# The sums of a graph attention kept row by row on VectorE, with the division given to GpSimd

## The reference

```
xl = (x @ Wl.T + bl).reshape(n, H, C)             # H = 4 heads of C = 32
...
p = jnp.exp(e - m[dst])
z = jax.ops.segment_sum(p, dst, num_segments=n)
alpha = p / (z[dst] + 1e-16)
out = jax.ops.segment_sum(xl[src] * alpha[:, :, None], dst, num_segments=n)
...
h = jax.nn.elu(h)                                  # then the second attention
```

## Time and profile before

| | |
|---|---|
| time, median of 3 runs | 6555.59 us (6553.88 to 6563.34) |
| span of the profiled execution, first to last instruction (no other time of its own is known) | 8635.1 us |
| DVE busy in the span | 4326.1 us (50%) |
| POOL busy | 4305.3 us (50%) |
| PE busy | 4016.2 us (47%) |
| ACT busy | 2282.2 us (26%) |
| mean granted TensorE clock | 0.650 |

### The profile page before, as it was taken

One profiled execution on the slowest core, in us unless ns is written; L12 is line 12 of the kernel. 1 busy time (PEld: TensorE's weight loads), 2 busy tenths in 40 slices (PEclk: granted clock), 3 DMA queues, 4 the chain that ended last, 5 costly groups with the idle time before them and its releaser, 6 DMA issues. The chain is left out here.

```text
span 8635.1 us, 76490 instructions
## 1 busy us (share of the span) xinstructions
PE 4016.2 (47%) x19708; PEld 2671.9 (31%) x19708; DVE 4326.1 (50%) x14882; ACT 2282.2 (26%) x5999; POOL 4305.3 (50%) x4026
## 2 busy tenths in 40 slices
PE   1111158312888825654563664342465476567000
PEld 0000034101555514443442443332344355233000
DVE  3010069301999944434432553565244698677553
ACT  0000000001777621110110333354111133799000
POOL 5777720575000046546555674774555100888577
PEclk8555589655999955555555555555666666798555
DMA  1111100000222222222222343343122144555222
GB/s 42 47 46 47 47 19 0 21 1 5 103 113 107 99 70 79 69 73 64 69 68 63 112 128 112 94 139 112 44 68 68 77 161 163 125 146 138 76 82 77
DMA packets 413612, 684.96 MB, mean 79 GB/s; under 512 B 283685, under 2 KB 290444, under 8 KB 407978
## 3 DMA queue, kind: packets, MB, share of 16 engines
q1 hardware_dynamic: 282410, 542.14, 17.7%
q0 software_dynamic: 130944, 140.05, 7.5%
HBM read 310.94 MB, written 373.78 MB: 79 GB/s over the span
## 5 line engine op out<-in xcount | busy, mean ns | idle before, releaser
L711 POOL DMA_INDIRECT G<-states,srcq x1568 | 1678.9, 1071 | 851.1 <-issue 479.5
L1133 DVE TENSOR_TENSOR_SCAN R<-same,R,G 128x28 f32<-128x28 f32 x4480 | 883.8, 265 | 622.1 <-issue 499.9
L1793 PE MATMUL PS<-ident,HH 128*128 128x128 f32 x2357 | 529.8, 376 | 1257.4 <-ACT AT L2063 373.2
L2063 ACT COPY AT<-PS 128x512 f32<-128x512 f32 (+1 forms) x494 | 283.7, 581 | 2467.3 <-remote 1375.1
L1793 PEld LDWEIGHTS PS<-ident,HH 128*128 128x128 f32 x2357 | 402.8, 205 | 1332.9 <-issue 409.9
L711 POOL DMA_INDIRECT EE<-node_info,srcq x392 | 394.4, 1006 | 545.0 <-DMA node_info<-XC 415.7
L1701 PE MATMUL PS<-R 128*128 128x392 f16 x784 | 283.0, 361 | 673.2 <-remote 375.7
L711 POOL DMA_INDIRECT G<-states,srci x392 | 406.7, 1038 | 321.0 <-ACT HH L2161 199.1
L1808 PEld LDWEIGHTS PS<-WD,AT 128*128 128x128 f32 x2358 | 505.8, 316 | 183.0 <-issue 182.7
L1808 PE MATMUL PS<-WD,AT 128*128 128x64 f32 x2358 | 560.6, 416 | 0.0
L824 POOL DMA_INDIRECT out_nodes<-O,dstq x392 | 430.9, 1099 | 188.2 <-issue 123.3
(11 more groups left out here) (412 smaller groups left out, 10157.6 us busy)
## 6 DMA issues: line engine op xcount, KB each, us to landing
states<-O SPq DMA_DIRECT2D x70, 896.0 KB, 3.6
HH<-states SPq DMA_DIRECT2D x56, 896.0 KB
total<-R SPq DMA_DIRECT2D x56, 896.0 KB
XB<-resid SPq DMA_DIRECT2D x42, 896.0 KB
states<-HH SPq DMA_DIRECT2D x28, 896.0 KB, 3.9
G<-states,srcq POOLq DMA_INDIRECT x1568
resid<-XB SPq DMA_DIRECT2D x28, 896.0 KB
xl_of_src<-O SPq DMA_DIRECT2D x14, 1792.0 KB
```

Of the source, the lines that this page charges most:

```text
L711: return pool.indirect_dma_start(to, None, table_, bass.IndirectOffsetOnAxis(ap=idx, axis=0), bounds_check=bound, oob_is_err=False).then_i ...
L1133: last = dve.tensor_tensor_scan(out=out_[:, order, f], data0=flags[:, order], data1=in_[:, order, f], initial=initial[:, f:f + 1], op0=ALU ...
L1793: last = pe.transpose(PS[:, 4 + k, q * P:(q + 1) * P], HH[:, b, (g * G4 + q) * D2:(g * G4 + q + 1) * D2], ident[:])
L2063: act.copy(AT[:, k, 0:n * P], PS[:, 4 + k, 0:n * P]).then_inc(s_copied, 1)
```

## The change

The turned layout goes. DVE weighs a chunk in place in G or XB, seven instructions of 128 x 512, and it does so one chunk ahead: `weigh(i + 1)`, then `sum_rows(i)`, then the seven elus of chunk i-1 in a row. `sum_rows` adds column by column, 28 instructions of 128 x 128, each waiting for the one before. R is now a pair of buffers, and the first column of a chunk takes its carry from the last column of the other. GpSimd divides in seven instructions of 128 x 512 (L869 of the changed program). The flags, their copies by ACT and two fills are gone. SP's program is untouched.

```diff
+            after("sum1")
+            for i in range(CHUNKS):
+                b = i % 2
+                if i >= 2:
+                    pool.wait_ge(s_st[b], before["sum1", "st"] + 16 * (i // 2))
+                    pool.wait_ge(s_turned, before["sum1", "group"] + GROUPS * (i - 1))
+                pool.wait_ge(s_scan, before["sum1", "scan"] + 1 + i)
+                for g in range(GROUPS):
+                    at = slice(g * G4 * D2, (g + 1) * G4 * D2)
+                    last = pool.tensor_tensor(head_rows(HH[:, b, at]), head_rows(R[:, b, at]), per_head(Ec, i * C + g * G4, G4), ALU.mult)
+                last.then_inc(s_ready, 1)
...
-            def weighted(i, b, between=None):
...
+            def weigh(i, b):
+
                 dve.wait_ge(s_ld[b], before["sum1", "ld"] + 16 * (i // 2 + 1))
...
+                for g in range(GROUPS):
+                    some = head_rows(XL[b][:, g * G4 * D2:(g + 1) * G4 * D2])
+                    last = tt(some, some, per_head(Ea, i * C + g * G4, G4), ALU.mult)
+                last.then_inc(s_weighed, 1)
+
+            def sum_rows(i, b):
+
                 if i >= 2:
...
+                    dve.wait_ge(s_ready, before["sum1", "ready"] + i - 1)
+                dve.wait_ge(s_weighed, i + 1)
+                for j in range(C):
+                    row_before = R[:, b, (j - 1) * D2:j * D2] if j else R[:, 1 - b, (C - 1) * D2:]
+                    row = dve.scalar_tensor_tensor(out=R[:, b, j * D2:(j + 1) * D2], in0=row_before, scalar=same[:, i * C + j:i * C + j + 1],
+                                                   in1=XL[b][:, j * D2:(j + 1) * D2], op0=ALU.mult, op1=ALU.add)
+                    if j < C - 1:
+                        step(row)
+                row.then_inc(s_scan, 1)
...
-            weighted(0, 0)
-            for i in range(1, CHUNKS):
-                weighted(i, i % 2, elus(i - 1, (i - 1) % 2))
+            weigh(0, 0)
+            for i in range(CHUNKS):
+                step.reset()
+                if i + 1 < CHUNKS:
+                    weigh(i + 1, (i + 1) % 2)
+                sum_rows(i, i % 2)
+                if i:
+                    for g in range(GROUPS):
+                        elu(i - 1, (i - 1) % 2, g)
```

More of the change, by code:

```diff
@@ L234, in build_program @@
         s_sm = sem("softmax_step")
[L235 to L239, removed]
+        s_weighed = sem("rows_weighed")
         s_last = sem("last_tails_known")
@@ L361, in build_program, with head_rows, per_head @@
         AHEAD = 2
+        def head_rows(t):
+            return t.rearrange("p (j h c) -> p j h c", h=HEADS, c=D2 // HEADS)
+        def per_head(e, first, n):
+            return e[:, :, first:first + n].rearrange("p h j -> p j h").unsqueeze(3).broadcast_to([P, n, HEADS, D2 // HEADS])
         XL = [t.rearrange("p b n -> p (b n)") for t in (G[:], XB[:])]
@@ L1497, in _ @@
             barrier()
-            def weighted(i, b, between=None):
-                step.reset()
+            def weigh(i, b):
                 dve.wait_ge(s_ld[b], before["sum1", "ld"] + 16 * (i // 2 + 1))
[L1504 to L1522, removed]
-                if i >= 2:
-                    dve.wait_ge(s_st[b], before["sum1", "st"] + 16 * (i // 2))
-                dve.wait_ge(s_scan, before["sum1", "scan"] + 1 + i)
[L1526 to L1530, removed]
@@ L1539, in elu @@
                                          op0=ALU.add, op1=ALU.max).then_inc(s_elu, 1)
[L1541 to L1545, removed]
-            dve.sem_inc(s_elu, AHEAD)
-            for k in range(2):
-                step(dve.memset(FLAGS[k], 0.0))
-            dve.nop().then_inc(s_flags, 1)
-            weighted(0, 0)
-            for i in range(1, CHUNKS):
-                weighted(i, i % 2, elus(i - 1, (i - 1) % 2))
+            dve.sem_inc(s_elu, AHEAD)
+            weigh(0, 0)
[7 more added lines that the diff above has]
+                        elu(i - 1, (i - 1) % 2, g)
             for g in range(GROUPS):
@@ L1926, in _ @@
             barrier()
-            pe.matmul(PS[:, 3, 0:D2], CARRY[:], FEATS[:, :, C - 1], start=True, stop=True).then_inc(s_carry, 1)
+            pe.matmul(PS[:, 3, 0:D2], CARRY[:], R[:, 1, (C - 1) * D2:], start=True, stop=True).then_inc(s_carry, 1)
             turn("sum1", CHUNKS, 0, 0, 1)
@@ L2190, in _ @@
                 act.sem_inc(s_rows[b], 32)
[L2192 to L2196, removed]
             def both_steps(i, it, b):
-                if i + 2 < CHUNKS:
-                    flags(i + 2)
                 for g in range(GROUPS + 2):
@@ L2205, in both_steps @@
                         second_operands("sum1", i, b, g - 2, it=it)
-            for i in range(2):
-                flags(i)
             for i in range(CHUNKS):
```

## The result

The changed kernel takes 6767.4 us (median of 4 runs, 6761.62 to 6774.58) against 6554.7 before (4 runs). The ratio is 1.033, with a 95% interval of 1.0313 to 1.0346: 213 us slower, where 180 were forecast.

The account below looks back on a forecast made before the run. DVE was taken to bound the stage. Turns of stall 15.1 + weighing 4.3 + rows 10.6 + elus 17 = 47.0 us against 30.9 made the stage 622 instead of 441.5: 6556 + 180 = 6736 us, range 6650 to 6830.

Parts of the forecast that it names:

- What bounds the stage: DVE bounds the stage before the change, busy 434 of 490 us, at 30.9 us a chunk.
- the saving of DVE's work: On DVE, 21.4 us a chunk removed and 14.9 added: 6.5 less by busy time, 90 us in all.
- The load is late: At a turn's first weighing, DVE waits for chunk i+2's load behind earlier products: 15.1 us, ends 11.1 and 20.2.
- The elus in a row: DVE's seven elus, with no other work between, go at PE's pace: 17 us a chunk, ends 14.3 and 21.5.
- the rival of the low clock: PE's clock stays low in every burst: elus 21.5 us instead of 17, twelve times, +54, 6790 us; chance 14%.
- the forecast stage: The whole stage, summed from the first load's landing: 622 us where it took 441.5, so +180.
- the forecast's own range: Range of kernel time for the main case, given 60%: 6700 to 6775 us.
- Weighing 4.3 and rows 10.6: DVE's added work a chunk: weighing in place 4.3 us, and 28 row sums 10.6 us, ends 9.0 and 10.9.
- GpSimd's division costs nothing on the path: GpSimd's seven division instructions, 0.6 to 1.59 us each, are hidden by a cover of 6.4 us each.
- The rival that GpSimd holds DVE up: GpSimd's division delays each of a turn's first two elus by up to 1.59 us: +38, 6774 us; chance 9%.
- The faster rival: At DVE's weighing the load isn't waited for: -27, 6528 us with elus at 14.3, +8 at 17; chance 6%.
- Carrying the stage's microseconds over in full: The stage's 180 us were added whole to the 6556 us median, though the profiled span is 8635 us.

Follow-up runs that it names:

- the two runs: Changed kernel with SP issuing the load and the store of divided sums before the earlier chunk's products, 6567.8 us; or with DVE's weighing in its own turn, 6571.0 us.
- another order: Changed kernel with weighing in its own turn, SP reordered and elus two turns behind, evenly spread: 6541.6 us dividing on GpSimd, 6519.5 us dividing on DVE.

## Why the prediction was right, point by point

- What bounds the stage, and that the saving of DVE's work (6.5 us a chunk) would not show: right. DVE's busy time in the stage fell from 411 us to 326, 85 less where 90 had been forecast, and the time rose.
- The load is late: right, and shown twice by taking the wait away. The stall was 16.1 us on the average of ten turns (161.4 us), not 15.1. From the first store's issue to the landing it was 12.1, with 11.8 forecast; the rest is the tail of the products, which was longer where PE ended its work at the lower clock: 4937.05 to 4943.35 is 6.3 us in the turn shown, and 3.3 had been taken from a stretch at the quick pace. Two of the eleven turns have this long tail, with stalls of 18.4 us; in the other nine the stall is 15.5 to 15.8, close to the forecast. This is the first term that was too small.
- The elus in a row: right in kind, and the second term that was too small. 17 was chosen between 14.3 and 21.5; it was 50.0 - 16.1 - 4.2 - 10.8 = 18.9, from 14.0 in the quickest turn to 21.7 in the slowest. In the turn shown PE was busy all the time and the clock stayed at the lower level, as the windows view has it (last three columns: clock, DMA share, GB/s); an earlier turn's burst ran at the higher one:

```profile
4920.00:4930.00 10.00, 10.00 (x38) 7.73 (x37) 3.85 (x5) 3.84 (x9) 3.28 (x4) 0.50 0.00 0
4830.00:4840.00 10.00, 10.00 (x66) 7.75 (x65) 5.91 (x9) 5.71 (x14) 3.76 (x4) 0.99 0.00 0
```

  So the rival of the low clock held in a part of the turns. Both terms together are 2.9 us a turn, 32 of the 36 us that the forecast stage (622) is short of 658. Both erred the same way, so the time, 6767, came out near the upper end of the forecast's own range of 6700 to 6775; no other part of the sum is off by more than 5 us.
- Weighing 4.3 and rows 10.6: measured 4.3 and 10.8.
- GpSimd's division costs nothing on the path: right for this kernel. An instruction takes 1.07 us undisturbed, inside the forecast's bounds of 0.6 and 1.59. The Trainium skill, GPSIMD Engine Reference, section "Performance versus the Vector engine", has 4497 ns for 2048 elements, from which the prediction had an estimated 1.1, and the trace agrees. The rival that GpSimd holds DVE up was seen in small: the tensor_scalars of the third and fourth elu take 0.75 and 1.17 us instead of 0.43, and PE's pace hides most of it.
- The faster rival, that the load is not waited for, needed elus under 16.4 us to beat the kernel before. With the load in time and the elus still in a row the two runs stand 0.3% above it, which is the side on which elus of some 18 us put them (17.7 us on the average in the one, 17.6 in the other).
- Carrying the stage's microseconds over in full although the profiled span was 2080 us longer than the timed runs: right; the stage grew by 216 and the median by 213. The traces also say where the old span's excess lay: ahead of the stage. The first weighing starts at 6876.6 us in it and at 4784.1 in the changed kernel's, 2092 us apart, while from the last elu to the end it is 1317 us in the one and 1318 in the other. What caused it is not shown.

## What to carry to other kernels

When work is moved earlier on one engine, look up what released its input: a queue that issues in order keeps the old distance, and a load that was a turn early becomes a load that is waited for. Work that follows another engine's pace needs other work between its pieces; seven elus set in a row cost some 100 us here with nothing else changed. And what work given to GpSimd is worth hangs on what DVE does beside it: in the same stage the division on GpSimd saved some 45 us where DVE had elus that waited for PE anyway, and cost 22 in another order (6541.6 against 6519.5).

## What the runs showed of the hardware

I had given a conflict of DVE and GpSimd 9%, and put it at two instructions a turn. Where their products meet, DVE's of 128 x 512 takes 1.56 us instead of 0.68 and GpSimd's 1.52 instead of 1.07. One after the other they would need 1.75, side by side 1.07. It is not only products of two tiles in SBUF that are held up: a row sum (two such tiles, L1528) took up to 1.04 us instead of 0.35 beside the division in the run with the elus between the rows, and in the changed kernel the first instruction of an elu (one such tile, L1539) up to 1.17 instead of 0.43, while its second, which reads PSUM and one such tile (L1541), never took more than its 0.75 (ns, shortest, median and longest; the first line is of the run with the elus between the rows):

```profile
L1528 DVE SCALAR_TENSOR_TENSOR R<-R,same,XB x196: 340/352/1043, 4805.2 to 5194.7; 128x128 f32<-128x128 f32 x196
...
L1539 DVE TENSOR_SCALAR SX<-SX x99: 227/428/1166, 4825.7 to 5456.0; 128x512 f32<-128x512 f32 x98, 128x128 f32<-128x128 f32 x1
...
L1541 DVE SCALAR_TENSOR_TENSOR AT<-PS,bias1c,SX x99: 350/751/753, 4826.1 to 5456.2; 128x512 f32<-128x512 f32 x98, 128x128 f32<-128x128 f32 x1
```

The Trainium skill, SBUF — State Buffer, section "SBUF: two separate sides", says that the shared port pair is held for a whole instruction and the loser is blocked; the trace agrees that two products take turns, though a pair goes by in a little less than the two lengths: in the run with the elus between the rows seven of DVE's beside seven of GpSimd's were through after 10.5 us (4857.24 to 4867.74), where 4.30 and 7.26, their times alone in the changed kernel, make 11.6.

Of two transfers of one queue the first was not left alone by the next: a load of 1.8 MB landed 6.7 us after its issue with another load behind it, and 8.3 us with three stores behind it.
